# Softplus as an absolute value, and the first sum of a block on VectorE, in a four-stage graph and Mamba kernel

## The reference

```python
h = relu(adj @ x @ gcn_w + gcn_b); h = layernorm(h) * ln_g + ln_b
xz = h @ w_in                                   # 512 columns xc, 512 columns z
u  = silu(causal_conv4(xc))
dbc = u @ w_xp                                  # 16 dt columns, 16 B, 16 C
dt = softplus(dbc[:, :16] @ w_dt + b_dt)        # 4096 x 512
# for each of 16 states n:
h_n[t] = exp(dt[t] * A[n]) * h_n[t-1] + dt[t] * u[t] * B[t, n]
y[t]  += C[t, n] * h_n[t]                       # summed over the 16 states
y = (y + u * D_skip) * silu(z); out = y @ w_out
```

## Time and profile before

| | us |
|---|---|
| median of 3 runs (2433.29 to 2436.95) | 2435.46 |
| the profiled execution, its own time | 2436.95 |
| its span | 2435.1 |
| busy over the span: PE | 2226.5 |
| DVE | 1864.9 |
| ACT | 1542.8 |
| POOL | 1132.5 |

### The profile page before, as it was taken

How to read it: one execution, slowest core, us unless ns; L and a number is a source line. 1 busy time by engine, 2 the same in 40 slices (tenths; PEclk the granted TensorE clock), 3 DMA queues, 4 the chain that set the end, 5 groups by cost and what they waited for, 6 DMA issues and landing times.

```text
span 2435.1 us, 26090 instructions
## 1 busy us (share of the span) xinstructions
PE 2226.5 (91%) x8852; PEld 1394.9 (57%) x8852; DVE 1864.9 (77%) x2135; ACT 1542.8 (63%) x2495; POOL 1132.5 (47%) x914
## 2 busy tenths in 40 slices
PE   7998999999999999988999989998999997765998
PEld 4444545454545456545766666666666663433886
DVE  5666868686777675323899899999999998996765
ACT  4677776767686755424676766667676756763444
POOL 2101212222221213302987888888887877891000
PEclk9999999999999999999999999999999998698999
DMA  5232332323333323232323232332333220113121
GB/s 212 94 125 95 104 110 90 121 78 121 94 108 102 112 87 122 88 104 96 121 96 113 96 113 87 107 119 88 122 99 117 90 89 24 53 43 113 35 78 43
DMA packets 116309, 238.05 MB, mean 98 GB/s; under 512 B 8226, under 2 KB 65954, under 8 KB 115794
## 3 DMA queue, kind: packets, MB, share of 16 engines
q1 hardware_dynamic: 107106, 204.00, 25.6%
q0 software_dynamic: 8528, 31.36, 3.7%
q10 hardware_dynamic: 544, 1.05, 0.1%
HBM read 216.06 MB, written 20.32 MB: 97 GB/s over the span
## 4 chain that ended last, share of the span: by engine, by line
PE 54%; DVE 13%; POOL 12%; ACT 11%; issue 9%; DMA 0%; DVEq 0%; ACTq 0%; SPq 0%; POOLq 0%
PE ps L637 13%; POOL dB L2234 8%; PE ps L679 6%; DVE h L1416 5%; PE ps L923 3%; PE ps L801 2%; DVE wgt L1109 2%; PE ps L775 2%; PE ps L907 2%; ACT wgt L1603 2%; DVE acc L1388 2%; POOL acc L2217 2%; POOL du L2230 2%; PE ps L705 1%; ACT L1601 1%
## 5 line engine op out<-in xcount | busy, mean ns | idle before, releaser
L2234 POOL TENSOR_TENSOR dB<-du,bc 128x512 f32<-128x512 f32 x512 | 656.3, 1304 | 78.9 <-DVE h L1416 76.3
L1416 DVE TENSOR_TENSOR_SCAN h<-ps,hst,dB 128x512 f32<-128x512 f32 x512 | 641.2, 1272 | 37.1 <-ACT ps L1603 26.7
L637 PE MATMUL ps<-wgt,msg 128*128 128x512 f32 x1024 | 503.1, 605 | 16.8 <-DVE wgt L1109 15.2
L1603 ACT ACTIVATE ps<-dt,cols 128x512 f32<-128x512 f32 x512 | 352.5, 689 | 235.0 <-DVE h L1416 233.2
L679 PE MATMUL ps<-raw,msg 128*128 128x256 f32 x1792 | 452.2, 389 | 0.9 <-ACT hb L1603 0.9
L923 PE MATMUL ps<-consts,h 128*128 128x128 f32 x2048 | 332.7, 290 | 83.0 <-DVE acc L1388 40.5
L923 PEld LDWEIGHTS ps<-consts,h 128*128 128x128 f32 x2048 | 256.4, 148 | 250.8 <-DVE acc L1388 89.3
L679 PEld LDWEIGHTS ps<-raw,msg 128*128 128x128 f32 x1792 | 331.4, 196 | 74.1 <-issue 39.3
L637 PEld LDWEIGHTS ps<-wgt,msg 128*128 128x128 f32 x1024 | 189.2, 193 | 224.5 <-issue 192.8
L1603 ACT ACTIVATE wgt<-wgt 128x1024 f32<-128x1024 f32 x256 | 258.6, 1047 | 66.4 <-DVE wgt L1102 64.0
L2217 POOL TENSOR_TENSOR acc<-acc,part 128x512 f32<-128x512 f32 x160 | 203.9, 1274 | 84.1 <-ACT part L1603 81.6
(11 more groups left out here) (317 smaller groups left out, 3488.9 us busy)
## 6 DMA issues: line engine op xcount, KB each, us to landing
raw<-in_adjT SPq DMA_DIRECT2D x256, 512.0 KB, 3.6
bc<-tmp_bc SPq DMA_DIRECT2D x64, 512.0 KB, 4.9
E<-tmp_bc POOLq DMA_DIRECT2D x32, 512.0 KB, 4.1
xb<-in_xT POOLq DMA_DIRECT2D x8, 512.0 KB, 4.7
tmp_x<-xb POOLq DMA_DIRECT2D x8, 512.0 KB, 4.8
x<-tmp_x SPq DMA_DIRECT2D x8, 512.0 KB, 5.2
tmp_x<-x SPq DMA_DIRECT2D x8, 512.0 KB, 4.3
raw<-tmp_xn SPq DMA_DIRECT2D x8, 512.0 KB, 4.0
```

The costliest lines, as they stand in the source:

```text
L637: x = e.matmul(P[d][:, :], msg[:, j, d * 128:(d + 1) * 128], wgt[g % NW][:, l, :], start=j == 0, stop=j == NJ - 1)
L1416: e.tensor_tensor_scan(hr[n % 3][:, m, :], PS[4 + k % 2].t[:, :], dBr[k % 4][:, :], hst[:, n % 16, m:m + 1], ALU.mult, ALU.add).then_inc(S ...
L1603: return e.activation(out, in_, func, bias=bias, scale=scale)
L2234: e.tensor_tensor(dBr[k % 4][:, :], du[:, m, :], bcr[i % 3][:, n % 2, :], ALU.mult).then_inc(S("dB"), 1)
```

## The change

Two things are edited. The sums of the first state (`n == 0`) for `s` = 1, 2, 3 go from ACT to DVE, as a multiply out of PSUM into `acc`; `s == 0` stays on ACT and `s == 1` of the last block stays on PE. And softplus is made in another way: ACT writes the biased value itself (Identity) instead of its Relu; the absolute value, Exp and Ln run over pairs of tiles, 128 x 1024, out of SBUF; and DVE takes the maximum with 0 in the operation that adds. The steps of `pre_b` on ACT stay the same in number, but the operations stand at other steps. On DVE the layernorm's multiply is one step earlier (step 7, it was 8), and all that follows stays.

```diff
 def adder(ib, n, s):
-    if s == 1 and ib == NB - 1:
-        return "tensor"
-    if n == 0:
-        return "scalar"
     if s == 0:
-        return "gpsimd" if n < 14 else "vector"
+        return "scalar" if n == 0 else "gpsimd" if n < 14 else "vector"
     if s == 1:
-        return "gpsimd" if 4 <= n < 12 else "vector"
+        return "tensor" if ib == NB - 1 else "gpsimd" if 4 <= n < 12 else "vector"
     return "vector"
...
 # DVE, pre_b
                 e.tensor_tensor(hb[:, :, :], hb[:, :, :], two(m.ps), ALU.subtract).then_inc(m.evac, 1)
-                yield from [None] * 6
+                yield from (None, None, None, None, None)
...
                 e.tensor_tensor(hb[:, :, :], hb[:, :, :], two(v.ps), ALU.mult).then_inc(v.evac, 1)
-                yield from [None] * 4
+                yield from [None] * 5
...
-                        w.wait_ge(S("relu1"), 4 * ib + m + 1)
-                        e.tensor_tensor(what, what, th1[:, :, :], ALU.add).then_inc(S("th1r"), 1)
+                        e.scalar_tensor_tensor(what, what, 0.0, th1[:, :, :], ALU.max, ALU.add).then_inc(S("th1r"), 1)
...
 # DVE, scan: gather
+                        if n == 0:
+                            if ib:
+                                w.wait_ge(gate_use(ib - 1, 3).full, gate_use(ib - 1, 3).n)
+                            e.tensor_scalar(acc[:, s, :], b.ps[:, :], c, None, ALU.mult).then_inc(b.evac, 1)
...
 # ACT, pre_b
-                for q in range(2):
-                    for m in (2 * q, 2 * q + 1):
-                        b, at = preb_use(ib, 11 + m), 12 * ib + 6 * q + m % 2
-                        yield
-                        w.wait_ge(b.full, b.n)
-                        act(dtt[p][:, m, :], b.ps[:, :], ACT.Relu, bias=col("bdt", m)).then_inc(S("relu1"), 1)
-                        yield
-                        w.wait_ge(S("th1r"), 4 * ib + 2 + q)
-                        act(th1[:, m % 2, :], b.ps[:, :], ACT.Abs, bias=col("bdt", m)).then_inc(b.evac, 1)
-                    yield
-                    for k in range(2):
-                        b = preb_use(ib, 11 + 2 * q + k)
-                        w.wait_ge(b.evac, b.n)
-                        act(th1[:, k, :], th1[:, k, :], ACT.Exp, scale=-1.0).then_inc(S("abs1"), 1)
-                        yield
-                    for k in range(2):
-                        w.wait_ge(S("abs1"), 4 * ib + 2 * q + k + 1)
-                        act(th1[:, k, :], th1[:, k, :], ACT.Ln, bias=1.0).then_inc(S("tanh1"), 1)
-                        yield
-                    yield
+                for m in range(4):
+                    b = preb_use(ib, 11 + m)
+                    yield
+                    w.wait_ge(b.full, b.n)
+                    act(dtt[p][:, m, :], b.ps[:, :], ACT.Identity, bias=col("bdt", m)).then_inc(b.evac, 1)
+                    yield
+                    if m % 2:
...
+                        w.wait_ge(S("th1r"), n_th)
+                        act(th1[:, :, :], dtt[p][:, m - 1:m + 1, :], ACT.Abs).then_inc(S("abs1"), 1)
                         yield
+                        w.wait_ge(S("abs1"), at + 1)
+                        act(th1[:, :, :], th1[:, :, :], ACT.Exp, scale=-1.0).then_inc(S("abs1"), 1)
                         yield
+                        w.wait_ge(S("abs1"), at + 2)
+                        act(th1[:, :, :], th1[:, :, :], ACT.Ln, bias=1.0).then_inc(S("tanh1"), 1)
+                        n_th += 1
+                        yield from (None, None, None, None)
```

More of the change, by code:

```diff
@@ L1316, in pre_b @@
                 e.tensor_tensor(hb[:, :, :], hb[:, :, :], two(v.ps), ALU.mult).then_inc(v.evac, 1)
-                yield from [None] * 4
+                yield from [None] * 5
+                n_th = 4 * ib
                 for m in range(4):
@@ L1334, in pre_b @@
                         yield
-                        w.wait_ge(S("tanh1"), 6 * ib + m // 2 + 1)
+                        n_th += 1
+                        w.wait_ge(S("tanh1"), n_th)
                         e.scalar_tensor_tensor(what, th1[:, :, :], 1.0, what, ALU.add, ALU.mult).then_inc(S("th1r"), 1)
@@ L1343, in pre_b @@
                         yield from [None] * 5
-                        w.wait_ge(S("tanh1"), 6 * ib + 2 + 2 * (m // 2 + 1))
-                        w.wait_ge(S("relu1"), 4 * ib + m + 1)
-                        e.tensor_tensor(what, what, th1[:, :, :], ALU.add).then_inc(S("th1r"), 1)
+                        n_th += 1
+                        w.wait_ge(S("tanh1"), n_th)
+                        e.scalar_tensor_tensor(what, what, 0.0, th1[:, :, :], ALU.max, ALU.add).then_inc(S("th1r"), 1)
                         yield
@@ L1383, in gather @@
                         w.wait_ge(made.evac, made.n)
-                        if j - 4 in HANDED:
-                            w.wait_ge(S("summed"), HANDED[j - 4] + 1)
-                        else:
-                            w.wait_ge(hT_use(j - 4).evac, hT_use(j - 4).n)
-                        e.scalar_tensor_tensor(acc[:, s, :], b.ps[:, :], c, acc[:, s, :], ALU.mult, ALU.add).then_inc(b.evac, 1)
+                        if n == 0:
+                            if ib:
+                                w.wait_ge(gate_use(ib - 1, 3).full, gate_use(ib - 1, 3).n)
+                            e.tensor_scalar(acc[:, s, :], b.ps[:, :], c, None, ALU.mult).then_inc(b.evac, 1)
+                        else:
+                            if j - 4 in HANDED:
+                                w.wait_ge(S("summed"), HANDED[j - 4] + 1)
+                            else:
+                                w.wait_ge(hT_use(j - 4).evac, hT_use(j - 4).n)
+                            e.scalar_tensor_tensor(acc[:, s, :], b.ps[:, :], c, acc[:, s, :], ALU.mult, ALU.add).then_inc(b.evac, 1)
                 def gates(ib):
@@ L1861, in pre_b @@
                             w.wait_ge(x.evac, x.n)
-                        w.wait_ge(S("th1r"), 4 * ib + m // 2)
+                        w.wait_ge(S("th1r"), n_th)
                         act(th1[:, :, :], u[p][:, m - 1:m + 1, :], ACT.Tanh).then_inc(S("tanh1"), 1)
                         yield from (None, None)
+                        n_th += 1
                         yield
@@ L1875, in pre_b @@
                 w.wait_ge(S("du"), 4 * (ib - 1))
-                for q in range(2):
-                    for m in (2 * q, 2 * q + 1):
-                        b, at = preb_use(ib, 11 + m), 12 * ib + 6 * q + m % 2
+                for m in range(4):
[5 more added lines that the diff above has]
+                    if m % 2:
+                        at = 4 * ib + 2 * (m // 2)
+                        w.wait_ge(b.evac, b.n)
+                        w.wait_ge(preb_use(ib, 10 + m).evac, preb_use(ib, 10 + m).n)
+                        w.wait_ge(S("th1r"), n_th)
+                        act(th1[:, :, :], dtt[p][:, m - 1:m + 1, :], ACT.Abs).then_inc(S("abs1"), 1)
                         yield
-                        w.wait_ge(b.full, b.n)
-                        act(dtt[p][:, m, :], b.ps[:, :], ACT.Relu, bias=col("bdt", m)).then_inc(S("relu1"), 1)
+                        w.wait_ge(S("abs1"), at + 1)
+                        act(th1[:, :, :], th1[:, :, :], ACT.Exp, scale=-1.0).then_inc(S("abs1"), 1)
                         yield
-                        w.wait_ge(S("th1r"), 4 * ib + 2 + q)
-                        act(th1[:, m % 2, :], b.ps[:, :], ACT.Abs, bias=col("bdt", m)).then_inc(b.evac, 1)
-                    yield
-                    for k in range(2):
-                        b = preb_use(ib, 11 + 2 * q + k)
-                        w.wait_ge(b.evac, b.n)
-                        act(th1[:, k, :], th1[:, k, :], ACT.Exp, scale=-1.0).then_inc(S("abs1"), 1)
-                        yield
-                    for k in range(2):
-                        w.wait_ge(S("abs1"), 4 * ib + 2 * q + k + 1)
-                        act(th1[:, k, :], th1[:, k, :], ACT.Ln, bias=1.0).then_inc(S("tanh1"), 1)
-                        yield
-                    yield
+                        w.wait_ge(S("abs1"), at + 2)
+                        act(th1[:, :, :], th1[:, :, :], ACT.Ln, bias=1.0).then_inc(S("tanh1"), 1)
+                        n_th += 1
+                        yield from (None, None, None, None)
                 b = preb_use(ib, 15)
```

## The result

| | us |
|---|---|
| changed kernel, median of 4 (2452.02 to 2457.14) | 2455.22 |
| kernel before beside it, median of 4 (2432.19 to 2436.95) | 2434.38 |
| ratio, 95% interval | 1.0084, 1.0066 to 1.0101 |
| profiled execution of the changed kernel, own time | 2455.74 |
| its span | 2453.8 |

The changed kernel is 0.84% slower; the medians differ by 20.8 us. Forecast were 2452 us and 0.7%, a difference of 16.3 us. ACT is busy for 1527.7 us, 15 less; DVE for 1878.5, 14 more.

The account below looks back on a forecast made before the run. DVE was taken as the chain through softplus to the border, PE from there to the layernorm. 7 x (0.98 + 0.43 + 0.4) + 3.1 + 0.5 = 16.3 us gave 2452 us, 0.7% slower; range 2438 to 2464.

Parts of the forecast that it names:

- Softplus, order, first pair: ACT's table load and Ln move ahead of exp 55, so scan 55 and the sum come later: +0.98 us a block.
- Second pair: Softplus's second pair, no table load: exp 60 comes behind Ln, delay grows from 0.98 to 1.41: +0.43 us a block.
- The layernorm's multiply: One step earlier on DVE, it waits 1.6 us for ACT; PE's transposes start later: +0.4 us a block, bounds 0 and 1.6.
- The sums of state 0: Multiplies moved to DVE at the borders, taken at 0.73 us, each adding 0.65: 3.1 us in all.
- the 7.9 us: DVE's time at a border from the first scan to the first sum, with three multiplies between them.
- the last border: Six scans ran without a gap and only two multiplies come in: +1.3 us.
- The 0.15 at each of the first four: Cost of the multiplies at each of the first four borders, after DVE's waits for PE take up part: 0.15 us.
- The fifth: Fifth border: the sum came 6.42 us after the first scan, so the multiplies cost +1.2 us there.
- at the sixth border it costs 0: DVE waited 1.74 us for an exp there, more room than at the others, so the multiplies cost 0.
- ACT's relief wins: Rival: ACT has less to do and DVE's waits of 2.71 us a block go; faster, 2421 us; chance 0.10.
- DVE is the bound all along: Rival: 1.95 us at each of seven borders and 1.3 at the last are exposed; 2464 us; chance 0.13.
- Nothing moves: Rival: PE is the true chain between blocks and DVE's lateness falls into PE's idle time; 2432 to 2441 us; chance 0.12.

Follow-up runs that it names:

- the pair's comparison: Sums of state 0 on DVE plus earlier layernorm multiply, old softplus (2445.99 us), held against the kernel before with only the earlier multiply (2435.98 us).
- the two pairs with the sums: Changed kernel with the multiply at its old step (2448.06 us), and changed kernel with the old softplus (2445.99 us); both keep the sums on DVE.
- the pair without them: Changed kernel with its sums back on ACT, so new softplus and earlier multiply together: 2449.36 us against 2434.84, ratio 1.0059.

## Why the prediction was right, and where it wasn't

*Softplus, order, first pair* (forecast +0.98 a block): +0.95 to +0.97 in six blocks, with the wait of 2.1 us where it was put. The kernel with the old operations and only Ln moved shows the cause, and putting Ln back takes it away. In the last block this term and the layernorm's belong together (2.58 and -0.43).

*Second pair* (+0.43): +0.36.

*The layernorm's multiply* (+0.4): +0.46 to +0.49 in four blocks. In two it was 1.01. There PE has no adjacency group (L679) between its matmuls L860 and L862, but transposes alone, and the transposes of the changed kernel wait for a sum of DVE twice. The changed kernel, in the block whose mean subtraction starts at 1745.49:

```profile
1754.41 0.66 PE L919 MATMUL ps<-consts,h 128*128 128x128 f32 x4 [0.25 <-DVE acc L1391]
...
1756.25 0.66 PE L919 MATMUL ps<-consts,h 128*128 128x128 f32 x4 [0.32 <-DVE acc L1391]
```

In the other blocks the 1.03 us of the adjacency group cover the second wait. DVE's own lateness is swallowed in these two blocks as well, since the convolution still waits 0.73 us. I took the blocks to repeat each other to 0.1 us and multiplied one by seven; from mean subtraction to mean subtraction they take between 134.8 and 136.9 us in the kernel before. That mis-sized the term, 2.8 for 3.5.

*The sums of state 0* (3.1): the multiply's price and the 7.9 us were right, and so was the last border (+1.31 for 1.3). The 0.15 at each of the first four came out as 0. The fifth was put too high (+0.63 for 1.2). The step that failed is "at the sixth border it costs 0": I took DVE's wait of 1.74 us for an exp for room that the kernel has there. It went with a clock of 0.71 in that one trace, and the border came out 1.5 us shorter, as it did with the sums on ACT. Where the same clock is held against the same clock (the pair's comparison), the sums cost 0.11 and 0.04 us at these two borders. The term measured 0.2 against the kernel before and 2.9 in the pair's comparison.

*What the sum left out.* 4.1 us of waits behind a fall of PE's clock and 1.8 in the last block. They happen to stand against the 2.9 by which the sums came out better and a start that was 2.2 earlier, so the total was nearer than its terms, by luck. Against the medians the sum is 4.5 us short. The waits go with the sums on DVE: 11 in the 36 ordinary borders (all but the last) of six traces with the sums there, none in the 42 of seven with the sums on ACT. How they come about is only partly seen. PE is idle for 1.90 to 1.98 us ahead of them, where it is 1.87 or 1.88 at the others; but ten borders with 1.97 or 1.98 us had no fall of the clock. What decides was not found.

*The rivals.* "ACT's relief wins" needed exp 55 at 1526.9 at the latest, on the old time scale; with Ln one exp later it comes about there, and even so the new softplus gains nothing. Part of that may be the 1 us that DVE's second sum then loses beside POOL. The relief of the 23 products alone brought nothing either (2438.49). The rule of the Trainium skill ("ScalarE: Activation LUTs", Rules for kernel authors) therefore didn't decide here: the multiply takes 0.73 us on DVE and took 0.68 on ACT, and moving it gained at no border that can be put down to it. Its drain of 1.38 us at a table switch (same page, What ACT_TABLE_LOAD costs) isn't in these traces either: 0.02 us lie between load and Ln. "DVE is the bound all along" (2464) was wrong, as the first four borders show: with the sums on DVE and the rest as before they cost between -0.23 and +0.06 us each. "Nothing moves" was wrong too.

*The interaction.* One by one the parts cost 13 us, together 20. Alone, the softplus got back 4.4 us at the first four borders and the multiply 1.5; with the sums on DVE nothing is got back there. These 5.9 us, read from single traces, are of the size of the 7 between the medians' ratios; that they are the whole account isn't shown. My theory in the middle of the work, one slack of DVE's waits that the parts share, held at the borders of the two pairs with the sums but fell with the pair without them. What the softplus got back goes with PE's clock staying up at a border, and it is of use only where PE's work ends last there; for what the multiply alone got back I have no cause. Why the clock stayed up at just ten of 28 borders stays open.

## What to carry to other kernels

Read the place of an operation in an engine's list before its length: 0.5 us of work saved a pair bought nothing, and a table load moved ahead of one exp cost 1 us a block. When a stretch repeats, check each repetition: here PE's order differed in two blocks and its clock at two borders, and both were taken for what the first block had shown. A long wait in one trace isn't room until a second trace of the same kernel has it too. And hold the parts' single costs with care where two engines end close together: here they added up to 0.54% and cost 0.84% together.

## What the runs showed of the hardware

Behind the border a wait of PE of 1.97 us was followed by matmuls at the lower clock level (1.88 us for the four that take 1.03) and one of 1.88 us never was. But ten waits of 1.97 or 1.98 us in the other traces were followed by matmuls at the upper level, so the length of the wait doesn't decide by itself. At the border, around the gates, the same kernel source can run at either level: the changed kernel had 1.00 at its first border in one execution and 0.83 in the other.

An addition of DVE out of two SBUF tiles and an operation of POOL that begin together don't share. In the kernel with the new softplus alone and Ln late, POOL begins first and DVE's sum takes 2.20 us in place of 1.22:

```profile
1541.14 1.26 POOL L2237 TENSOR_TENSOR dB<-du,bc 128x512 f32<-128x512 f32 x1
```

```profile
1541.29 2.20 DVE L1348 SCALAR_TENSOR_TENSOR dt<-dt,th 128x1024 f32<-128x1024 f32 x1
```

In the kernel before, DVE's sum takes 1.22 us and POOL's product 2.34 in place of 1.26:

```profile
1539.03 2.34 POOL L2234 TENSOR_TENSOR dB<-du,bc 128x512 f32<-128x512 f32 x1
```

Where POOL began 0.15 us ahead, DVE's sum is about 1 us longer; where both began within 0.01 us of each other, POOL's product is. This agrees with the Trainium skill ("SBUF — State Buffer", Who interferes with whom), which has DVE and GpSimd contend for a shared pair of ports, an exclusive lock, when DVE has two inputs in SBUF and GpSimd reads SBUF too. None of my terms had it.
